# Second layer of a four-layer graph network: 93 of 440 value blocks gathered later, edge one-hots on ScalarE, scaling on two engines

## Chip, cores and metric

The kernel runs on one core of one Trainium2 chip. The metric is device time in microseconds, the median of the runs.

## What is computed

The reference is a network of four layers over 3125 nodes with 256 features and 53,125 edges. Each layer adds a graph part, a mixing part and a feed-forward part to `x`. The change touches only the graph part of the second layer. This is attention over the edges, with 4 heads of 64 features:

```
q, k, v = xn @ Wq + bq (+ query), xn @ Wk + bk, xn @ Wv + bv     # one row of 256 per node
score   = sum over a head of q[dst] * (k[src] + rel_w[relation])   # per edge and head
alpha   = softmax of score over the edges of one dst
out     = segment_sum(alpha * v[src], dst) @ Wo + bo, then a norm with gamma, beta
```

The second line is written from the kernel's own steps; edges are sorted by their destination.

## The kernel before

**The steps.** The sorted edges are cut into `STEPS` = 440 blocks of `W` = 128 edges, one edge per partition; 8 steps are a group (`GROUP`), of which there are 55, and two steps are a pair. A step touches one tile of `P` = 125 destination nodes; there are `NT` = 25 tiles. The function `gnn1` runs five phases one behind the other, with a barrier of all engines between them:

1. `gnn1_front` writes the table `keyval1` to HBM: 3125 rows of 512 numbers, the 256 of the key and then the 256 of the value.
2. `edge_scores` (its tiles are named `g_sc_...` in the profile). GpSimd gathers with an indirect DMA the 128 rows of a step, 2 KB each, into one of 14 slots of `rows` (L3404). SyncE copies the value half of each slot, 128 KB, to a table `kept1` in HBM (L3367), and fetches per group 256 KB of `which` and 250 KB of `near` (L3357, L3358). TensorE spreads the queries of the step's tile over its edges (L3423, three matmuls in bf16) and the relation weights (L3426, L3427). VectorE takes three passes over a pair: add (L3451), multiply (L3455), sum over each head (L3459). GpSimd may fill a slot again when the scores of its pair are made (`scored`) and its value half is stored (`stashed`). Between the pairs TensorE, VectorE and ScalarE also run the layer's mixing part (`mix`, L3117 to L3316), which is spread over the turns.
3. `segment_softmax` (`g_sm_...`) works on the scores alone, through two round trips to HBM. GpSimd has nothing to do in it.
4. `weighted_sums` (`g_sp_...`). SyncE loads the stored values of a step from `kept1` into one of 24 slots (L3618). GpSimd multiplies a pair by `alpha`, 128 partitions by 512 numbers (L3639). ScalarE copies the 8 alphas of a pair beside it (L3630). VectorE makes the one-hot matrix of a step by a comparison (L3657), 8 steps ahead, TensorE multiplies the one-hots and the values (L3650, one f32 matmul of 260 columns, which the profile shows as two), and VectorE adds the bank to the step's tile in `total` (L3665). The comparison reads a ramp that was put into PSUM. One add waits for the one before it (`v.wait_ge(added, s)`), since both may go to one tile.
5. `gnn1_tail` (`g_tail_...`) divides, applies `Wo` and the norm.

The order on every engine is the order in which the code is written; there is no planner. The loops are these:

Of the kernel before, what the change touches and what calls it, by code (L numbers as in the profile page):

```python
# [6 lines left out]
I32 = mybir.dt.int32  # L7
# [3311 lines left out]
def edge_scores(core, name, table, kept, query, relation, factor, scores, heads):  # L3319

# [10 lines left out]
    with Phase(nc, name) as ph:  # L3331
# [8 lines left out]
        const, scaled, numbered, apart, which_set, chain_sem = (ph.sem(n) for n in ("const", "scaled", "numbered", "apart", "which_set", "chain"))  # L3340
        expanded, shifted, multiplied, scored = (ph.sem(n) for n in ("expanded", "shifted", "multiplied", "scored"))
        banks = [ph.ps_pair(f"pair{k}") for k in range(PAIR_BANKS)]
        mix = MemoryMix(core, ph)
        block = ph.block()

        @block.sync
        def _(sp):
            for half in (slice(0, 64), slice(64, 128)):
                sp.dma_start(number[half, :], a["c_types"]).then_inc(const, 16)
                sp.dma_start(rel[half, :], a[relation]).then_inc(const, 16)  # L3350
            mix.load(sp)

            def mark(g):
                if g >= HELD:
                    sp.wait_ge(expanded, GROUP * (g - HELD + 1))
                mine = slice(g * GROUP * W, (g + 1) * GROUP * W)
                sp.dma_start(which[:, g % HELD, :], core.kind_rows[mine].partition_broadcast(128)).then_inc(kind_in[g % HELD], 16)  # L3357
                sp.dma_start(near[:, g % HELD, :], core.near_rows[g, 0:P, :]).then_inc(near_in[g % HELD], 16)  # L3358

            for g in range(HELD):  # L3360
                mark(g)
            for s in range(STEPS):
                k = s % SLOTS
                if s % GROUP == GROUP // 2 and HELD <= s // GROUP + 2 < GROUPS:
                    mark(s // GROUP + 2)
                sp.wait_ge(gathered[k], 16 * (s // SLOTS + 1))
                sp.dma_start(kept[s * W:(s + 1) * W, :], rows[:, k, D:2 * D]).then_inc(stashed[k], 16)  # L3367
            for k in range(SLOTS):
                sp.wait_ge(stashed[k], 16 * ((STEPS - 1 - k) // SLOTS + 1))

        @block.scalar
        def _(act):
# [23 lines left out]

        @block.gpsimd
        def _(pool):
            for s in range(STEPS):
                k = s % SLOTS  # L3400
                if s >= SLOTS:
                    pool.wait_ge(scored, (s - SLOTS) // 2 + 1)
                    pool.wait_ge(stashed[k], 16 * (s // SLOTS))
# [26 lines left out]

        @block.vector
        def _(v):
            nc.vector.memset(one[:], 1.0).then_inc(numbered, 1)
            v.wait_ge(const, 64)
            nc.vector.tensor_scalar(minus[:], number[:], -1.0, None, ALU.mult).then_inc(numbered, 1)
            link = Chain(v, chain_sem).link
# [25 lines left out]
            v.wait_ge(scored, PAIRS)  # L3462


def segment_softmax(core, name, scores, factor, alpha, heads):

# [7 lines left out]
    with Phase(nc, name) as ph:  # L3474
# [19 lines left out]
        banks = [ph.ps(f"bank{i}") for i in range((nv + per - 1) // per)]  # L3494
        turns = [ph.ps(f"turn{i}") for i in range(4)]
        block = ph.block()

        @block.sync
        def _(sp):
# [93 lines left out]
def weighted_sums(core, name, source, alpha, heads, total, own, values):  # L3593

    nc = core.nc
    SLOTS, BANKS, RING, AHEAD = 24, 7, 16, 8
    PAIRS = STEPS // 2  # L3600
    dim = D // heads
    with Phase(nc, name) as ph:
        rows = ph.sb("rows", [W, SLOTS, D + heads])
        same = ph.sb("same", [W, RING, P])
        loaded = [ph.sem(f"loaded{k}") for k in range(SLOTS)]
        cleared, ramped, same_set, scaled, beside, summed, added = (ph.sem(n) for n in ("cleared", "ramped", "same_set", "scaled", "beside", "summed", "added"))
        own_in = ph.sem("own_in")
        banks = [ph.ps(f"bank{k}") for k in range(BANKS)]
        ramp = ph.ps("ramp")
        block = ph.block()  # L3610

        @block.sync
        def _(sp):
            for s in range(STEPS):
                k = s % SLOTS
                if s >= SLOTS:
                    sp.wait_ge(summed, s - SLOTS + 1)
                sp.dma_start(rows[:, k, 0:D], source[s * W:(s + 1) * W, :]).then_inc(loaded[k], 16)  # L3618
                if s % GROUP == GROUP - 1 and s // GROUP < NT:
                    t = s // GROUP  # L3620
                    node_dma(sp, own[:, t, :], nodes(values)[:, t, :], own_in)
            sp.wait_ge(own_in, 32 * NT)

        @block.scalar
        def _(act):
            for pair in range(PAIRS):
                if 2 * pair >= SLOTS:
                    act.wait_ge(summed, 2 * pair + 2 - SLOTS)
                k = 2 * pair % SLOTS
                nc.scalar.activation(rows[:, k:k + 2, D:D + heads], alpha[:, 2 * pair:2 * pair + 2, :], ACT.Copy).then_inc(beside, 1)  # L3630

        @block.gpsimd
        def _(pool):
            for pair in range(PAIRS):
                for s in (2 * pair, 2 * pair + 1):
                    pool.wait_ge(loaded[s % SLOTS], 16 * (s // SLOTS + 1))
                k = 2 * pair % SLOTS
                mine = rows[:, k:k + 2, 0:D].rearrange("p k (h d) -> p k h d", h=heads)
                nc.gpsimd.tensor_tensor(mine, mine, alpha[:, 2 * pair:2 * pair + 2, :].unsqueeze(3).to_broadcast([W, 2, heads, dim]), ALU.mult).then_inc(scaled, 1)  # L3639

        @block.tensor
        def _(pe):
            for s in range(STEPS):
                if s % 2 == 0:
                    pe.wait_ge(scaled, s // 2 + 1)
                    pe.wait_ge(beside, s // 2 + 1)
                pe.wait_ge(same_set, s + 1)
                if s >= BANKS:
                    pe.wait_ge(added, s - BANKS + 1)
                nc.tensor.matmul(banks[s % BANKS][0:P, 0:D + heads], same[:, s % RING, :], rows[:, s % SLOTS, :], start=True, stop=True).then_inc(summed, 1)  # L3650

        @block.vector
        def _(v):
            def compare(s):
                if s >= RING:
                    v.wait_ge(summed, s - RING + 1)
                nc.vector.tensor_scalar(same[:, s % RING, :], ramp[:, 0:P], core.local[:, s:s + 1], None, ALU.is_equal).then_inc(same_set, 1)  # L3657

            def add(s):
                tile = tiles.at(s)  # L3660
                there = total[:, bass.ds(tile, 1), :]
                v.lower_ap(there)
                v.wait_ge(added, s)
                v.wait_ge(summed, s + 1)
                nc.vector.tensor_tensor(there, there, banks[s % BANKS][0:P, 0:D + heads].unsqueeze(1), ALU.add).then_inc(added, 1)  # L3665

            nc.vector.tensor_copy(ramp[:, 0:P], core.ramp[:, 0:P]).then_inc(ramped, 1)
            nc.vector.memset(total[:], 0.0).then_inc(cleared, 1)
            v.wait_ge(ramped, 1)
# [3 lines left out]
            for s in range(AHEAD):  # L3673
                compare(s)
# [282 lines left out]
def gnn1(core):  # L3957
# [2 lines left out]
    table, kept = core.table("keyval1", N, 2 * D), core.table("kept1", STEPS * W, D)  # L3960
    values = table[:, D:2 * D]
    with Phase(nc, "g1") as whole:
        alpha = whole.sb("alpha", [W, STEPS, heads])
        with Phase(nc, "g1b") as outer:
            scores = outer.sb("scores", [W, heads, STEPS])
            with Phase(nc, "g1q") as scope:
                parts = scope.sb("parts", [P, 3, NT, D], BF16)
                gnn1_front(core, table, parts)
                edge_scores(core, "g1_sc", table, kept, parts, "L1_gnn_rel_w", 0.2, scores, heads)
            segment_softmax(core, "g1_sm", scores, dim ** -0.5, alpha, heads)  # L3970
        own, total = whole.sb("own", [P, NT, D]), whole.sb("total", [P, NT, D + heads])
        weighted_sums(core, "g1_sp", kept, alpha, heads, total, own, values)
        gnn1_tail(core, own, total, heads)


# [557 lines left out]
```

## Time and profile before

| what | value |
|---|---|
| runs | 5380.28, 5381.34 and 5816.96 us; median 5381.34 us |
| profiled execution, own time | 5367.56 us |
| its span | 5365.8 us |
| busy in the span | TensorE 77%, VectorE 58%, ScalarE 31%, GpSimd 48% |
| `edge_scores` | from 1609 to 2267 us |
| `segment_softmax` | from 2267 to 2337 us |
| `weighted_sums` | from 2337 to 2619 us |

The phases run one behind the other, so time saved inside one of the last three phases of this table is saved in the whole. An engine's busy share counts overlapping instructions once. For an indirect DMA the busy time on GpSimd is the time in which it prepares the transfer; the data land later. "Idle before" in a group of instructions is the time for which the engine stood still ahead of them, with what ended it.

### The profile page before, as it was taken

The numbers are of one execution on the slowest core, as the hardware profiler recorded it, in microseconds if no ns is written. First come the engines' busy times: TensorE is split into PE (matmuls) and PEld (weight loads), VectorE is DVE, ScalarE is ACT, GpSimd is POOL, SyncE is SP. The second block draws the span as 40 slices with busy tenths as digits, with TensorE's granted clock in tenths as the row PEclk, the third lists the DMA queues.
The fourth block names the chain that finished last, engine by engine and source line by source line (L and its number), as shares of the span: only waits on it lengthen the run. The fifth ranks groups of instructions, "written<-read, shape, count | busy, mean of one in ns | idle before, by whom it ended". The sixth has DMA issues, their size and how long they took to land. (4 is left out here: it accounts for less than half of the span.)

```text
span 5365.8 us, 71878 instructions
## 1 busy us (share of the span) xinstructions
PE 4148.9 (77%) x19209; PEld 3079.2 (57%) x19209; DVE 3099.9 (58%) x7473; ACT 1672.2 (31%) x3813; POOL 2601.8 (48%) x2664
## 2 busy tenths in 40 slices
PE   1689997888976877559859678887499997888674
PEld 1357775656843544334548556666277765566564
DVE  5525546721057788779851467898522225688843
ACT  1345554532231322211333211000233334344221
POOL 1377775502206676548625367775000006777444
PEclk9799998988986777679969889888699999999877
DMA  5344447730028999857332344444100003333434
GB/s 176 117 150 156 155 148 229 220 104 27 31 87 281 328 329 320 268 157 230 91 115 71 95 128 122 122 120 89 48 0 0 0 5 116 103 101 97 94 101 128
DMA packets 463670, 705.71 MB, mean 132 GB/s; under 512 B 70819, under 2 KB 340649, under 8 KB 462923
## 3 DMA queue, kind: packets, MB, share of 16 engines
q0 software_dynamic: 115216, 335.54, 20.8%
q1 hardware_dynamic: 327133, 344.61, 20.5%
q10 hardware_dynamic: 20978, 21.42, 1.3%
q8 instruction: 162, 2.65, 0.2%
q14 instruction: 181, 1.48, 0.1%
HBM read 496.93 MB, written 205.25 MB: 131 GB/s over the span
## 5 line engine op out<-in xcount | busy, mean ns | idle before, releaser
L830 POOL DMA_INDIRECT m_rows<-support,edge x440 | 445.6, 1013 | 878.9 <-POOLq L129 737.1
L3404 POOL DMA_INDIRECT g_sc_rows<-keyval,src_at x440 | 430.3, 978 | 321.0 <-POOLq L129 107.3
L4014 POOL DMA_INDIRECT g_sp_rows<-h,src_at x440 | 469.8, 1068 | 145.9 <-issue 97.2
L2210 POOL DMA_INDIRECT messages<-m_rows,place_at x440 | 429.8, 977 | 154.8 <-issue 96.0
L3423 PE MATMUL g_sc_pair<-g1q_parts,g_sc_near 125*128 x1320 | 289.5, 341 | 145.9 <-DVE g_sc_rows L3455 112.6
L4063 PE MATMUL g_sp_bank<-g_sp_rows,g_sp_same 128*125 128x264 f32 x880 | 287.8, 435 | 73.3 <-DVE g_total L4203 68.7
L1391 DVE SCALAR_TENSOR_TENSOR x<-f_y,f_comb,x 125x256 f32 x200 | 96.8, 484 | 377.9 <-PE f_y L1208 377.9
L851 PE MATMUL m_half<-m_rows,m_marks 128*125 128x256 f32 x880 | 240.8, 408 | 70.3 <-issue 33.6
L3639 POOL TENSOR_TENSOR g_sp_rows<-g_sp_rows,g_alpha 128x512 f32<-128x512 f32 x220 | 225.0, 1043 | 126.2 <-DMA g_sp_rows<-kept 122.7
L1250 ACT ACTIVATE f_hid<-f_h,f_shift,f_scale 128x375 f32<-128x375 f32 (+1 forms) x320 | 195.5, 611 | 288.9 <-PE f_h L1187 283.2
L3650 PE MATMUL g_sp_bank<-g_sp_rows,g_sp_same 128*125 128x260 f32 x880 | 263.5, 421 | 17.2 <-POOL g_sp_rows L3639 10.7
L889 DVE TENSOR_TENSOR g_total<-g_total,m_half 125x256 f32 x440 | 184.7, 420 | 137.8 <-PE m_half L851 120.7
L955 PE MATMUL g_sums_bank<-g_sums_rows,g_sums_marks 128*125 128x256 f32 x880 | 203.1, 387 | 52.4 <-ACT g_sums_marks L946 52.0
L3423 PEld LDWEIGHTS g_sc_pair<-g1q_parts,g_sc_near 125*128 125x128 bf16 x1320 | 126.6, 109 | 197.0 <-issue 161.6
L851 PEld LDWEIGHTS m_half<-m_rows,m_marks 128*125 128x125 f32 x880 | 157.5, 198 | 131.7 <-issue 72.8
L4063 PEld LDWEIGHTS g_sp_bank<-g_sp_rows,g_sp_same 128*125 128x125 f32 x880 | 155.4, 203 | 123.6 <-DVE g_sp_rows L4190 45.3
L3451 DVE TENSOR_TENSOR g_sc_rows<-g_sc_rows,g_sc_pair 128x512 f32<-128x512 f32 x220 | 150.8, 685 | 122.7 <-PE g_sc_pair L3427 53.8
L3650 PEld LDWEIGHTS g_sp_bank<-g_sp_rows,g_sp_same 128*125 128x125 f32 x880 | 132.7, 188 | 147.9 <-issue 98.0
L955 PEld LDWEIGHTS g_sums_bank<-g_sums_rows,g_sums_marks 128*125 128x125 f32 x880 | 162.5, 189 | 92.8 <-ACT g_sums_marks L946 70.3
L973 DVE TENSOR_TENSOR g_total<-g_total,g_sums_bank 125x256 f32 x440 | 185.3, 421 | 48.5 <-PE g_sums_bank L955 34.2
L2244 ACT ACTIVATE m_rows<-m_message,edge 128x256 f32<-128x256 f32 x440 | 178.9, 472 | 82.9 <-PE m_message L2229 82.6
L1457 POOL DMA_INDIRECT xnT<-sorted_rows,f_from_at x160 | 158.9, 993 | 91.0 <-issue 41.8
(734 smaller groups left out, 10425.7 us busy)
## 6 DMA issues: line engine op xcount, KB each, us to landing
g_sums_rows<-messages SPq DMA_DIRECT2D x110, 520.0 KB
kept<-g_sc_rows SPq DMA_DIRECT2D x440, 128.0 KB, 9.1
g_sp_rows<-kept SPq DMA_DIRECT2D x440, 128.0 KB, 2.6
answer_rows<-zero ACTq DMA_DIRECT2D x1, 14592.0 KB
g_sc_which<-kind_rows SPq DMA_DIRECT2D x55, 256.0 KB
m_local_in<-local_rows SPq DMA_DIRECT2D x55, 252.0 KB
near_rows<-m_near SPq DMA_DIRECT2D x55, 252.0 KB
g_sc_near<-near_rows SPq DMA_DIRECT2D x55, 250.0 KB
```

Of the source, the lines that this page charges most:

```text
L830: nc.gpsimd.indirect_dma_start(self.rows[:, k, :], None, self.table, bass.IndirectOffsetOnAxis(ap=core.far_at[:, s:s + 1], axis=0)).then_i ...
L851: nc.tensor.matmul(self.halves[s % slots], self.mark(s), self.rows[:, s % self.SLOTS, :], start=True, stop=True).then_inc(self.summed, 1)
L955: nc.tensor.matmul(halves[s % len(halves)], marks[:, s // GROUP % HELD, s % GROUP, :], rows[:, s % SLOTS, 0:D], start=True, stop=True).the ...
L973: nc.vector.tensor_tensor(there, there, halves[s % len(halves)].unsqueeze(1), ALU.add).then_inc(added, 1)
L1250: nc.scalar.activation(hid[layer][:, i % 2, mo, 0:n], hbank[q % HR][:, 0:n], func, scale=scale[layer][:, g, mo:mo + 1], bias=shift[layer][ ...
L2210: nc.gpsimd.indirect_dma_start(core.messages, bass.IndirectOffsetOnAxis(ap=core.place_at[:, s:s + 1], axis=0), self.rows[:, k, :], None).t ...
L3404: nc.gpsimd.indirect_dma_start(rows[:, k, :], None, table, bass.IndirectOffsetOnAxis(ap=core.src_at[:, s:s + 1], axis=0)).then_inc(gathere ...
L3423: nc.tensor.matmul(banks[pair % PAIR_BANKS][:, s % 2, 0:D], near[:, g % HELD, k * W:(k + 1) * W], query[:, i, bass.ds(tile, 1), :].rearran ...
L3639: nc.gpsimd.tensor_tensor(mine, mine, alpha[:, 2 * pair:2 * pair + 2, :].unsqueeze(3).to_broadcast([W, 2, heads, dim]), ALU.mult).then_inc ...
L3650: nc.tensor.matmul(banks[s % BANKS][0:P, 0:D + heads], same[:, s % RING, :], rows[:, s % SLOTS, :], start=True, stop=True).then_inc(summed, 1)
L4014: nc.gpsimd.indirect_dma_start(self.rows[:, k, :], None, self.table, bass.IndirectOffsetOnAxis(ap=core.src_at[:, s:s + 1], axis=0)).then_i ...
L4063: nc.tensor.matmul(self.banks[s % self.BANKS][0:P, 0:D + self.heads], self.same[:, g % 2, k, :], self.rows[:, s % self.SLOTS, :], start=Tr ...
```

## The change

A new class `Late` names 93 steps: 0 to 23, and from there each sixth (29, 35, ..., 437: 69 of them). For these `edge_scores` gathers only the key half (128 KB instead of 256) and stores nothing; the table is read as 6250 rows of 256 numbers, with indices that VectorE makes at the start of the phase. The values of steps 0 to 23 are gathered by GpSimd during `segment_softmax` into space that `own` takes later, those of the 69 others during `weighted_sums`, each 18 steps ahead of GpSimd's own scaling. The slots there are loaded for steps 24 to 47 at once.

In `weighted_sums` the one-hots are no longer compared by VectorE. ScalarE makes eight squares of (node number - local destination) and one `Relu(1 - square)` over the group. VectorE scales each third pair (pairs 2, 5, 8, ...: 73 in all), GpSimd the other 147. There are 8 banks instead of 7. The diff, cut to what matters:

```
+class Late:
+    EARLY, EVERY = 24, 6
+        self.steps = [t for t in range(STEPS) if t < self.EARLY or t % self.EVERY == self.EVERY - 1]
...
 edge_scores, sync:
+                if s not in late.index:
+                    sp.wait_ge(gathered[k], 16 * (s // SLOTS + 1))
+                    sp.dma_start(kept[s * W:(s + 1) * W, :], rows[:, k, D:2 * D]).then_inc(stashed[k], 16)
 edge_scores, gpsimd:
+            pool.wait_ge(late_set, 2)
...
                     pool.wait_ge(scored, (s - SLOTS) // 2 + 1)
+                    if s - SLOTS not in late.index:
+                        pool.wait_ge(stashed[k], 16 * late.stashes(SLOTS, k, s))
+                if s in late.index:
+                    nc.gpsimd.indirect_dma_start(rows[:, k, 0:D], None, halves, bass.IndirectOffsetOnAxis(ap=late.key(s), axis=0)).then_inc(gathered[k], 16)
+                    continue
...
-    SLOTS, BANKS, RING, AHEAD = 24, 7, 16, 8
+    SLOTS, BANKS, HELD = 24, 8, 3
+    AHEAD, SOONER, THIRD = 18, 3, 3
...
+        def on_vector(pair):
+            return pair % THIRD == THIRD - 1
...
+        def scale(eng, pair):
+            rows_in(eng, pair)
+            mine = there(pair)[:, :, 0:D].rearrange("p k (h d) -> p k h d", h=heads)
+            return eng.tensor_tensor(mine, mine, alpha[:, 2 * pair:2 * pair + 2, :].unsqueeze(3).to_broadcast([W, 2, heads, dim]), ALU.mult)
...
 weighted_sums, scalar:
+                for k in range(GROUP):
+                    s = g * GROUP + k
+                    ins = nc.scalar.activation(mine[:, k, :], core.ramp[:, 0:P], ACT.Square, bias=minus_local[:, s:s + 1])
+                ins.then_inc(apart, 1)
+                act.wait_ge(apart, g + 1)
+                nc.scalar.activation(mine, mine, ACT.Relu, scale=-1.0, bias=one[:, 0:1]).then_inc(same_set, 1)
...
 weighted_sums, gpsimd:
+                if s >= 2 * SLOTS:
+                    pool.wait_ge(summed, s - SLOTS + 1)
+                nc.gpsimd.indirect_dma_start(rows[:, k, 0:D], None, halves, bass.IndirectOffsetOnAxis(ap=late.value(s), axis=0)).then_inc(loaded[k], 16)
...
             for pair in range(PAIRS):
+                for s in (2 * pair + AHEAD, 2 * pair + 1 + AHEAD):
+                    if late.EARLY + AHEAD <= s < STEPS and s in late.index:
+                        gather(s)
+                if not on_vector(pair):
+                    scale(nc.gpsimd, pair).then_inc(pool_scaled, 1)
...
 weighted_sums, vector:
+            for pair in range(SOONER):
+                scale_third(pair)
             for s in range(STEPS):
-                if s + AHEAD < STEPS:
-                    compare(s + AHEAD)
                 add(s)
+                if s % 2 == 0:
+                    scale_third(s // 2 + SOONER)
...
 gnn1:
+        def gather_early(pool):
+            for s in range(late.EARLY):
+                nc.gpsimd.indirect_dma_start(early[:, s, 0:D], None, halves, bass.IndirectOffsetOnAxis(ap=late.value(s), axis=0)).then_inc(early_in, 16)
```

GpSimd in `edge_scores`: where one run of 440 gathers of 512 numbers per row stood, there stand now 24 of 256 numbers, and then one short gather behind each five long ones.

```order
+L3433 DMA g_sc_rows<-keyval,g_late_at 128x256 x24
+L3435 DMA g_sc_rows<-keyval,src_at 128x512 x5
+L3433 DMA g_sc_rows<-keyval,g_late_at 128x256
+L3435 DMA g_sc_rows<-keyval,src_at 128x512 x5
+L3433 DMA g_sc_rows<-keyval,g_late_at 128x256
```

The count of gathers on GpSimd stays at 440 in this phase; only what they move changes.

VectorE at the start of `weighted_sums`, before the change (L809 is the reading of the tile number that an add needs; `g_sp_same` are the one-hots, `g_sp_bank` is what TensorE made):

```order
 L3667 COPY g_sp_ramp<-ramp 128x125
 L3668 MEMSET g_total 125x6500
 L806 TENSOR_LOAD step_tile
 L3657 TENSOR_SCALAR g_sp_same<-g_sp_ramp,local 128x125 x9
 L809 ISA
 L3665 TENSOR_TENSOR g_total<-g_total,g_sp_bank 125x260
 L3657 TENSOR_SCALAR g_sp_same<-g_sp_ramp,local 128x125
```

and after it (`g_own` is the space of the values of steps 0 to 23):

```order
+L3762 TENSOR_SCALAR g_sp_minus_local<-local 128x440
+L3763 MEMSET g_total 125x6500
+L806 TENSOR_LOAD step_tile
+L3675 TENSOR_TENSOR g_own<-g_own,g_alpha 128x2x256
+L809 ISA
+L3755 TENSOR_TENSOR g_total<-g_total,g_sp_bank 125x260
```

One comparison between every two adds is gone; one multiplication of 512 numbers, with both inputs in SBUF, stands behind each six adds.

GpSimd in `weighted_sums`: where 220 multiplications stood in one run (L3639), there are now pairs of them, with a gather between.

```order
+L3721 DMA g_sp_rows<-keyval,g_late_at 128x256 x3
+L3675 TENSOR_TENSOR g_own<-g_own,g_alpha 128x2x256 x8
+L3675 TENSOR_TENSOR g_sp_rows<-g_sp_rows,g_alpha 128x2x256 x2
+L3721 DMA g_sp_rows<-keyval,g_late_at 128x256
+L3675 TENSOR_TENSOR g_sp_rows<-g_sp_rows,g_alpha 128x2x256 x2
```

## Rows read from the trace of the kernel before

**Rows 1.** The page: the span.

```profile
span 5365.8 us, 71878 instructions
```

**Rows 2.** Windows: PE, PEld, DVE, ACT, POOL busy (instructions), PE clock, DMA share, GB/s.

```profile
1640.00:1700.00 60.00, 39.94 (x243) 26.32 (x242) 55.31 (x89) 9.47 (x10) 39.37 (x38) 0.69 0.84 262
1700.00:1950.00 250.00, 198.44 (x1178) 132.79 (x1176) 189.93 (x340) 71.32 (x111) 171.62 (x181) 0.77 0.97 331
1950.00:2250.00 300.00, 209.64 (x1190) 129.46 (x1190) 262.42 (x433) 81.17 (x107) 203.23 (x207) 0.68 0.95 314
2267.00:2337.00 70.00, 11.25 (x38) 7.94 (x38) 32.63 (x76) 8.63 (x10) 0.00 (x0) 0.52 0.18 55
2346.00:2618.00 272.00, 263.37 (x880) 132.50 (x880) 264.98 (x878) 43.37 (x208) 219.88 (x215) 0.99 0.72 218
```

**Rows 3.** Groups, 1600 to 2270 us: busy us, mean ns, idle before and its releasers.

```profile
L3404 POOL DMA_INDIRECT g_sc_rows<-keyval,src_at x440 | 430.3, 978 | 321.0 <-POOLq L129 107.3 <-issue 93.5 <-DMA kept<-g_sc_rows 62.3
```

**Rows 4.** DMA view, 1600 to 2270 us: queue, packets, MB, share of 16 engines.

```profile
q0 software_dynamic: 35200, 115.37, 52.1%
q1 hardware_dynamic: 80184, 88.02, 39.9%
```

**Rows 5.** Timeline, both ends of `edge_scores`: start us, us, engine, line [idle before].

```profile
1625.74 0.94 POOL L3404 DMA_INDIRECT g_sc_rows<-keyval,src_at  x1 [0.30 <-issue]
1631.88 0.82 PE L3423 MATMUL g_sc_pair<-g1q_parts,g_sc_near 125*128 x3 [27.59 <-DMA g_sc_near<-near_rows]
...
1640.85 1.23 POOL L3404 DMA_INDIRECT g_sc_rows<-keyval,src_at  x1 [14.17 <-DMA kept<-g_sc_rows]
...
2252.49 0.95 POOL L3404 DMA_INDIRECT g_sc_rows<-keyval,src_at  x1 [0.30 <-issue]
...
2262.16 0.69 DVE L3451 TENSOR_TENSOR g_sc_rows<-g_sc_rows,g_sc_pair 128x512 f32<-128x512 f32 x1 [0.27 <-issue]
...
2264.55 1.27 DVE L3459 TENSOR_REDUCE g1b_scores<-g_sc_rows 128x8 f32<-128x512 f32 x2
```

**Rows 6.** Groups of `weighted_sums`, and of matmuls in the first layer's sums.

```profile
L3650 PE MATMUL g_sp_bank<-g_sp_rows,g_sp_same 128*125 128x260 f32 x880 | 263.5, 421 | 17.2 <-POOL g_sp_rows L3639 10.7 <-DVE g_total L3665 0.9
L3639 POOL TENSOR_TENSOR g_sp_rows<-g_sp_rows,g_alpha 128x512 f32<-128x512 f32 x220 | 225.0, 1043 | 126.2 <-DMA g_sp_rows<-kept 122.7
L3665 DVE TENSOR_TENSOR g_total<-g_total,g_sp_bank 125x260 f32 x438 | 182.3, 416 | 0.7 <-issue 0.2 <-PE g_sp_bank L3650 0.2
L3657 DVE TENSOR_SCALAR g_sp_same<-g_sp_ramp,local 128x125 f32<-128x125 f32 x440 | 150.5, 344 | 7.0 <-DVE g_total L3668 0.8 <-PE g_sp_bank L3650 0.5 <-issue 0.2
...
L955 PE MATMUL g_sums_bank<-g_sums_rows,g_sums_marks 128*125 128x256 f32 x880 | 203.1, 387 | 52.4 <-ACT g_sums_marks L946 52.0
```

**Rows 7.** Timeline of `weighted_sums`: runs on GpSimd and VectorE, whole time and count.

```profile
2339.15 5.47 DVE L3668 MEMSET g_total<- 125x6500 f32 x1 [1.34 <-issue]
...
2466.66 13.05 POOL L3639 TENSOR_TENSOR g_sp_rows<-g_sp_rows,g_alpha 128x512 f32<-128x512 f32 x13 [0.25 <-DMA g_sp_rows<-kept]
...
2614.17 4.09 DVE L3665 TENSOR_TENSOR g_total<-g_total,g_sp_bank 125x260 f32 x9
```

**Rows 8.** Timeline of `gnn1_tail`: VectorE with GpSimd idle, and with it at work.

```profile
2660.03 0.42 DVE L3948 TENSOR_TENSOR x<-x,g_tail_beta 125x256 f32<-125x256 f32 x1
2660.37 0.42 DVE L3915 TENSOR_TENSOR g_own<-g_tail_out,xw 125x256 f32<-125x256 f32 x1
...
2660.83 0.72 POOL L3848 TENSOR_TENSOR g_own<-g_own,g_tail_gamma 125x256 f32<-125x256 f32 x1 [0.94 <-ACT g_own L3900]
2661.03 0.80 DVE L3948 TENSOR_TENSOR x<-x,g_tail_beta 125x256 f32<-125x256 f32 x1
```

**Rows 9.** Groups on ScalarE: nearest rows to its new work.

```profile
L946 ACT ACTIVATE g_sums_marks<-g_sums_marks,g_sums_one 128x1000 f32<-128x1000 f32 x55 | 62.1, 1128 | 1.8
L3193 ACT ACTIVATE g_sc_mkvrow<-g_sc_mkvrow 125x128 f32<-125x128 f32 x25 | 7.5, 300 | 0.0
L3630 ACT ACTIVATE g_sp_rows<-g_alpha 128x8 f32<-128x8 f32 x220 | 44.7, 208 | 220.5 <-PE g_sp_bank L3650 219.3 <-PEq L129 1.2
```

More of the change, by code:

```diff
@@ L3316, in dve_turn, with __init__, key, value @@
                 nc.vector.tensor_tensor(self.mid[:, k, :], self.banks[t % 2][0:P, D:2 * D], self.b[:], ALU.add).then_inc(self.taken, 1)
-def edge_scores(core, name, table, kept, query, relation, factor, scores, heads):
+class Late:
+    EARLY, EVERY = 24, 6
+    def __init__(self, scope):
+        self.steps = [t for t in range(STEPS) if t < self.EARLY or t % self.EVERY == self.EVERY - 1]
+        self.at = scope.sb("late_at", [W, 2, len(self.steps)], I32)
+        self.index = {t: j for j, t in enumerate(self.steps)}
+    def key(self, t):
+        return self.at[:, 0, self.index[t]:self.index[t] + 1]
+    def value(self, t):
+        return self.at[:, 1, self.index[t]:self.index[t] + 1]
+    def stashes(self, slots, k, until):
+        return len([t for t in range(k, until, slots) if t not in self.index])
+def edge_scores(core, name, table, kept, query, relation, factor, scores, heads, late):
     nc, a = core.nc, core.a
@@ L3342, in edge_scores @@
         banks = [ph.ps_pair(f"pair{k}") for k in range(PAIR_BANKS)]
+        count, first = len(late.steps), next(t for t in late.steps if t >= late.EARLY)
+        twice, late_set = ph.sb("twice", [W, count]), ph.sem("late_set")
+        halves = table.rearrange("n (k d) -> (n k) d", k=2)
         mix = MemoryMix(core, ph)
@@ L3607, in weighted_sums, with there, rows_in @@
         own_in = ph.sem("own_in")
         banks = [ph.ps(f"bank{k}") for k in range(BANKS)]
-        ramp = ph.ps("ramp")
         block = ph.block()
+        def there(pair):
+            s = 2 * pair
+            return early[:, s:s + 2] if s < late.EARLY else rows[:, s % SLOTS:s % SLOTS + 2]
+        def on_vector(pair):
+            return pair % THIRD == THIRD - 1
+        def rows_in(eng, pair):
+            for s in (2 * pair, 2 * pair + 1):
+                if s < late.EARLY:
+                    eng.wait_ge(early_in, 16 * late.EARLY)
+                else:
+                    eng.wait_ge(loaded[s % SLOTS], 16 * (s // SLOTS))
@@ L3625, in _, with match @@
         def _(act):
[L3626 to L3630, printed above, removed]
+            def match(g):
+                mine = same[:, g % HELD]
+                if g >= HELD:
+                    act.wait_ge(summed, GROUP * (g - HELD + 1))
+                for k in range(GROUP):
[4 more added lines that the diff above has]
+                nc.scalar.activation(mine, mine, ACT.Relu, scale=-1.0, bias=one[:, 0:1]).then_inc(same_set, 1)
@@ L3632, in _, with put_beside @@
+            def put_beside(g):
+                for pair in range(g * GROUP // 2, (g + 1) * GROUP // 2):
+                    if 2 * pair >= late.EARLY + SLOTS:
+                        act.wait_ge(summed, 2 * pair + 2 - SLOTS)
+                    nc.scalar.activation(there(pair)[:, :, D:D + heads], alpha[:, 2 * pair:2 * pair + 2, :], ACT.Copy).then_inc(beside, 1)
+            act.wait_ge(placed, 2)
+            for g in range(GROUPS):
+                match(g)
+                put_beside(g)
         @block.gpsimd
@@ L3643, in _ @@
             for s in range(STEPS):
+                pair = s // 2
                 if s % 2 == 0:
-                    pe.wait_ge(scaled, s // 2 + 1)
-                    pe.wait_ge(beside, s // 2 + 1)
-                pe.wait_ge(same_set, s + 1)
+                    mine = len([q for q in range(pair + 1) if on_vector(q) == on_vector(pair)])
+                    pe.wait_ge(dve_scaled if on_vector(pair) else pool_scaled, mine)
+                    pe.wait_ge(beside, pair + 1)
+                if s % GROUP == 0:
+                    pe.wait_ge(same_set, s // GROUP + 1)
```

94 lines of the change are left out of this document (52 added, 42 removed).

## The prediction

> **What bounds the kernel now.** I read the page first for the whole span, 5365.8 us [rows 1], then the windows over the second layer's phases, then the groups and waits inside them, and last the timeline where a pace had to be read. The profiled execution took 5367.56 us, which is 13.8 us under the median of the runs, 5381.34; I sum differences on the profiled one and put them on the median.
>
> In `edge_scores` the DMA engines are busy for 97% of 1700 to 1950 us and 95% of 1950 to 2250 [rows 2]. But nothing else is far off. GpSimd issued 181 gathers in the 250 us of the first stretch, one per 1.381 us, and 207 in the 300 us of the second, one per 1.449. Its own floor is 1.25 us: 0.95 for a gather and 0.30 of idle time behind it [rows 5]. VectorE is busy for 189.93/181 = 1.05 us per step in the first stretch and 262.42/207 = 1.27 in the second; from 1640 to 1700 it is busy 55.31 of 60 us with the DMA at 84% [rows 2]. Of GpSimd's time 93.5 us are its own gaps; of the 62.3 us behind the stores [rows 3], 14.17 are one wait at the start [rows 5]. So DMA limits the middle of the phase, VectorE its first 60 us, and the two together its second half.
>
> In `weighted_sums` VectorE is busy 264.98 of 272 us and waits for nobody, 0.7 and 7.0 us in all [rows 2, 6]. TensorE looks as full, 263.37 us, but it only spreads: the same matmuls, four columns shorter, were busy 203.1 us in the first layer's sums [rows 6]. The phase's pace is 272/440 = 0.618 us per step, 3.7 us for six.
>
> **The change in `edge_scores`.** A step moves 262 KB (128 rows of 2 KB) in, 131 KB out, and (256 + 250) KB/8, some 65 KB, of marks: 458 KB. Check: 331 GB/s by 1.381 us is 457 KB [rows 2]. A late step moves 196 KB. Six steps with one late are 5 x 458 + 196 = 2486 KB, 414 per step, 9.6% less. Bytes are the right measure: per MB the gather queue with 2 KB rows uses 52.1%/115.37 = 0.452% and the other queue, mostly 1 KB rows, 39.9%/88.02 = 0.453% [rows 4]; halving a row does not spoil it.
>
> - Start. The first matmul waits 27.59 us for the first `near`, behind the first gathers, and gather 15 waits 14.17 us until 1640.85 [rows 5]. The first 14 gathers move half and nothing is stored, 14 x 262 KB = 3.7 MB less in the 31 us. GpSimd's wait for the new indices (six small VectorE instructions, some 2 us) delays gathers that nobody wants yet: nothing. VectorE must still do its first pair, so I take -5 (0 to -14).
> - 1640 to 1700: VectorE, at 92%, is the limit: 0.
> - 1700 to 1950: at 331 GB/s, 414 KB take 1.25 us, which is also GpSimd's floor. Two limits at one value never both hold, so I take the middle, 1.31: 181 x 0.07 = -13 (0 to 181 x 0.13 = -24).
> - 1950 to 2250: 414/314 = 1.32 by DMA, 1.27 by VectorE, whose bursts of mixing work can't be filled in later. I take 1.37: 207 x 0.08 = -16 (-5 to 207 x 0.13 = -27).
> - End: from the last gather at 2252.49 to its pair at 2262.16 are 9.7 us [rows 5], with less in the queues some 3 less (0 to -6).
>
> Sum -37 us (-5 to -71).
>
> **`segment_softmax`.** 24 gathers by 1.25 us are 30 us on a GpSimd that did nothing for 70 us, and 3.1 MB on DMA engines at 18% [rows 2]: hidden. The small round trips may meet them: +2 (0 to +6). If that cover were gone, it would be 30 us.
>
> **`weighted_sums`**, per six steps, since the pattern repeats every six.
>
> - VectorE loses the comparisons. An add alone is bound to the one before: nine in 4.09 us, (4.09 - 0.42)/8 = 0.459 us [rows 7]. Six are 2.75. One scaling is a pass over 512 numbers: two such passes took 1.27 us, 0.68 each [rows 5], so one adds 0.59. Sum 3.34.
> - GpSimd: 13 scalings took 13.05 us, 1.0 each [rows 7]. Two, and one gather at 1.25, are 3.25.
> - ScalarE: 8 squares at 0.300 (the nearest row, 128 columns), one wide `Relu` at 1.128, 4 copies at 0.208: 4.36 us for eight steps, 3.27 for six [rows 9]. It works up to two groups ahead, so it hides.
> - TensorE: 203.1/440 = 0.46 per step, 2.8 [rows 6].
> - DMA: 0.72 busy [rows 2], and 3.1 MB have gone into the softmax. The 18 steps between a gather and its scaling by GpSimd leave about 10 steps (6 us) before VectorE wants it, against 9.7 us of landing in a full phase [rows 5]; at 0.72 the queues are short, so I put nothing on it.
>
> So everything would fit into 3.34, were it not for what these two engines do to each other. In the tail VectorE's add of 256 numbers with both inputs in SBUF took 0.42 us with GpSimd idle, and 0.80 when GpSimd's multiplication was under way: it ended 0.28 us behind it. The add with one input in PSUM took 0.42 [rows 8]. Before the change VectorE had no instruction with two SBUF inputs in this phase. Now it has 73. GpSimd scales for 2.0 of each 3.3 us, so a scaling of VectorE meets one in 6 cases of 10 and waits half of it: +0.3 us. If it then goes ahead of GpSimd's second scaling it holds that up by 0.59, in about 3 to 4 cases of 10: +0.2 on 3.25. The longer of the two is 3.64, with a little for unevenness 3.6 to 3.65; against 3.7 I take -0.08 by 73.3 = -6 us.
>
> The Trainium skill ("SBUF — State Buffer", section "Who interferes with whom") says that a VectorE instruction with two SBUF inputs contends with a GpSimd instruction that reads SBUF, and that the one that starts first keeps the shared port for its whole length. By that rule the trace agrees, with 0.42 against 0.80 us. Taken at its worst it gives the third rival's time.
>
> The bounds: below, 3.34, that is -0.36 x 73.3 = -26; above, VectorE waits for a whole scaling each time, 3.34 + 1.04 = 4.38, that is +0.68 x 73.3 = +50. The start is bound by the 5.47 us clearing of `total` [rows 7] as before, and TensorE's first step comes no later: 0.
>
> **The sum**: -37 + 2 - 6 = -41. 5367.56 - 41 = 5326.6 for a profiled execution, 5381 - 41 = 5340 for the median.
>
> **The rivals.**
>
> - *All of it shows.* The saved bytes turn into time to the limits above (-71), and the two scalings fall beside the gathers (-26): -97, 5284. For it: DMA at 95 to 97%. Against: GpSimd's floor stands at the same 1.25, and VectorE's 88% in the second half. Chance 0.13.
> - *The transfer was hidden anyway.* VectorE's bursts and GpSimd's issue take over at once in `edge_scores`, -8, and `weighted_sums` comes out even, with +2 in the softmax: 5375. For it: TensorE's and VectorE's waits on each other in the mixing part. Against: 93.5 us of GpSimd's gaps are the plain 0.30, so it ran unhindered for most gathers. Chance 0.18.
> - *The port decides.* VectorE's scaling waits for a whole one of GpSimd each time, as both run in one rhythm of six steps: +50, with -37 and +2 this is +15, 5396, slower than before. It decides from 3.7 + 35/73.3 = 4.18 us per six steps on. For it: a repeating order has no chance in it, it either always meets or never. Against: when VectorE waits, GpSimd runs on into its gather, which leaves the next meeting open. Chance 0.09.
>
> The forecast has 0.60, with a range of its own from 5320 to 5358.
>
> **How the numbers follow.** The range takes in the second rival (5375) and most of the first (5284), and leaves out most of the third: 5290 to 5382. A measurement of this kernel can tell about 2%, 107 us, from no change. Faster by that needs 5274, beyond even the first rival by 10: 0.05. Slower by it needs 5489, out of reach but for a fault that I don't see, such as gathers that land late for each of 69 pairs at over 1 us: 0.03. The same: 0.92.
>
> **What would show it.** In the trace of the changed kernel: the last gather of `edge_scores` some 35 us earlier, with 1.3 us per gather from 1700 on and the DMA share still over 0.9; waits behind `kept` nearly gone from GpSimd's; the softmax at 70 to 73 us; VectorE's scaling with a mean over 0.9 us instead of 0.68, some at 0.68 and some near 1.5; GpSimd's scaling over 1.04 in the mean; 0.60 us per step. Wrong would be: 0.56 per step with scalings at 0.68 (no meeting), a wait of VectorE on a gather, ScalarE as TensorE's releaser in `weighted_sums`, or a pace of `edge_scores` above 1.38.

## The result and the profile after

The changed kernel takes 5455.61 us in the median of 4 runs (5452.73 to 5461.37), the kernel before 5382.36: a ratio of 1.0131, with a 95% interval from 1.0117 to 1.0145. It is 73 us slower. One of the four runs of the kernel before, 5816.96 us, is in a slower state that some executions show, and the ratio leaves it out. I had forecast 5340 us, in a range up to 5382.

| phase | before | after | forecast |
|---|---|---|---|
| `edge_scores`, first gather to last score | 655.7 us | 624.3 us | -37 |
| `segment_softmax`, with its barrier | 69.9 us | 71.5 us | +2 |
| `weighted_sums`, clearing of `total` to last add | 279.1 us | 381.6 us | -6 |

The three differences are -31, +2 and +103, together +73. (The two profiled executions lie 85 us apart; 10 of it stand ahead of these phases, where the programs are the same, and 1 is the wait of the first gather for the new indices, which the first row leaves out. The first row goes from the start of the first gather to the start of the last score.)

The page's first lines after the change, then the windows over the same phases (span, then busy time of PE, PEld, DVE, ACT and POOL with instructions, PE clock, DMA share, GB/s):

```profile
span 5450.9 us, 71363 instructions
PE 4141.2 (76%) x19209; PEld 3135.2 (58%) x19209; DVE 3176.9 (58%) x7113; ACT 1843.8 (34%) x4308; POOL 2622.5 (48%) x2684
```

```profile
1700.00:1950.00 250.00, 198.73 (x1231) 134.54 (x1231) 205.48 (x367) 73.04 (x112) 181.97 (x191) 0.82 0.97 321
1950.00:2235.00 285.00, 206.64 (x1190) 129.37 (x1190) 253.28 (x421) 78.53 (x105) 196.55 (x202) 0.70 0.92 289
2247.00:2318.00 71.00, 11.47 (x38) 7.96 (x38) 32.71 (x76) 8.63 (x10) 25.52 (x24) 0.50 0.32 98
2327.00:2703.00 376.00, 255.11 (x874) 187.05 (x872) 347.25 (x514) 208.99 (x689) 211.00 (x209) 0.86 0.51 149
```

Against [rows 2]: the first stretch has 191 gathers in 250 us, 1.309 us each, where it had 1.381; the second 202 in 285, 1.41 where it had 1.449. The softmax hides its 24 gathers. The last row is the surprise: VectorE has 364 instructions less than in [rows 2] and is busy 82 us longer. TensorE's granted clock is 0.86 there, where it was 0.99; in e1 below, where TensorE's long waits are gone, it is 0.99 again.

The groups of `weighted_sums` say with what (answering to [rows 6]; busy us, mean ns, idle before and its releasers):

```profile
L3745 PE MATMUL g_sp_bank<-g_sp_rows,g_sp_same 128*125 128x260 f32 x832 | 243.4, 453 | 112.2 <-DVE g_sp_rows L3675 112.2
L3755 DVE TENSOR_TENSOR g_total<-g_total,g_sp_bank 125x260 f32 x440 | 185.9, 423 | 27.8 <-PE g_sp_bank L3745 12.5 <-DVE g_total L3755 3.3
...
L3675 DVE TENSOR_TENSOR g_sp_rows<-g_sp_rows,g_alpha 128x512 f32<-128x512 f32 x69 | 164.0, 2377 | 0.0
L3675 POOL TENSOR_TENSOR g_sp_rows<-g_sp_rows,g_alpha 128x512 f32<-128x512 f32 x139 | 142.0, 1047 | 1.4
L3699 ACT ACTIVATE g_sp_same<-ramp,g_sp_minus_local 128x125 f32<-128x125 f32 x440 | 133.4, 386 | 146.5 <-PE g_sp_bank L3745 145.3 <-DVE g_sp_minus_local L3762 1.2
...
L3721 POOL DMA_INDIRECT g_sp_rows<-keyval,g_late_at x69 | 68.1, 987 | 186.7 <-PE g_sp_bank L3745 146.8 <-POOLq L129 39.1 <-issue 0.8
```

A pass of VectorE over 512 numbers took 0.68 us in [rows 5]. Its scalings take 2377 ns in the mean. GpSimd's are as they were, 1047 ns. The timeline shows one cycle of six steps (start, duration, engine and line; several instructions in one row have their count behind x):

```profile
2456.03 0.99 POOL L3721 DMA_INDIRECT g_sp_rows<-keyval,g_late_at  x1 [2.03 <-PE g_sp_bank L3745]
2457.04 2.04 POOL L3675 TENSOR_TENSOR g_sp_rows<-g_sp_rows,g_alpha 128x512 f32<-128x512 f32 x2
2457.11 2.53 DVE L3675 TENSOR_TENSOR g_sp_rows<-g_sp_rows,g_alpha 128x512 f32<-128x512 f32 x1
...
2459.57 2.70 DVE L3755 TENSOR_TENSOR g_total<-g_total,g_sp_bank 125x260 f32 x6
...
2459.70 4.56 PE L3745 MATMUL g_sp_bank<-g_sp_rows,g_sp_same 128*125 128x260 f32 x12 [2.19 <-DVE g_sp_rows L3675]
...
2461.11 0.98 POOL L3721 DMA_INDIRECT g_sp_rows<-keyval,g_late_at  x1 [2.03 <-PE g_sp_bank L3745]
2462.12 2.05 POOL L3675 TENSOR_TENSOR g_sp_rows<-g_sp_rows,g_alpha 128x512 f32<-128x512 f32 x2
2462.19 2.53 DVE L3675 TENSOR_TENSOR g_sp_rows<-g_sp_rows,g_alpha 128x512 f32<-128x512 f32 x1
```

VectorE starts its scaling at 2457.11, 0.07 us behind GpSimd's first, and ends it at 2459.64. GpSimd's two scalings end at 2459.08; the rest, 0.56 us, is the scaling itself. So VectorE does not get in between the two. The next cycle follows 5.08 us later with the same lengths, to 0.01 us. In the record of the whole phase 65 of VectorE's 73 scalings are long, and each of the 65 ends 0.55 or 0.56 us behind the last of the GpSimd scalings that it met. Even clearer is the start of the phase, where GpSimd has ten scalings in a row:

```profile
2322.75 8.04 POOL L3675 TENSOR_TENSOR g_own<-g_own,g_alpha 128x512 f32<-128x512 f32 x8
2326.64 6.70 DVE L3675 TENSOR_TENSOR g_own<-g_own,g_alpha 128x512 f32<-128x512 f32 x1 [0.76 <-DVE g_total L3763]
2330.76 2.03 POOL L3675 TENSOR_TENSOR g_sp_rows<-g_sp_rows,g_alpha 128x512 f32<-128x512 f32 x2
```

The scaling that VectorE began in the fourth of them ended at 2333.34, 0.55 us behind the tenth.

The cycle can be added up from the rows above. VectorE's scaling ends at 2459.64. TensorE, which waited for it, starts 0.06 us later, the gather 1.41 us after that, and GpSimd's scalings 1.01 us after the gather. They take 2.05 us, and VectorE's next scaling ends 0.55 us behind them: 5.08 us. The code says why the gather comes just there. The gather of step t waits until TensorE has done step t - 24, and because 24 slots are four times the period of six, that step is always the second of a pair that VectorE scales.

My theory after this: (a) VectorE's instruction with two SBUF inputs does not get in before the end of a whole back-to-back run of GpSimd; (b) the meeting is no chance: TensorE waits for VectorE's scaling, GpSimd's gather waits for a slot that TensorE frees with the second step of that same pair, and the two scalings follow the gather, just when VectorE has done its six adds. The rivals: the gather's wait for its slot alone makes the cycle; the eight or six banks do; or VectorE loses against any scaling whatever the phase.

### The profile page after: what moved, and what is told of

Read it like the earlier page. It is cut to its first block and busy times, and to the rows that moved or that the text cites. A ratio compares the mean times of both kernels' runs of the same rounds, so it can differ in the third digit from the quotient of the medians.

```text
span 5450.9 us, 71363 instructions
## 1 busy us (share of the span) xinstructions
PE 4141.2 (76%) x19209; PEld 3135.2 (58%) x19209; DVE 3176.9 (58%) x7113; ACT 1843.8 (34%) x4308; POOL 2622.5 (48%) x2684
## 5 line engine op out<-in xcount | busy, mean ns | idle before, releaser
L3435 POOL DMA_INDIRECT g_sc_rows<-keyval,src_at x347 | 334.7, 965 | 141.9 <-issue 78.7
L3745 PE MATMUL g_sp_bank<-g_sp_rows,g_sp_same 128*125 128x260 f32 x832 | 243.4, 453 | 112.2 <-DVE g_sp_rows L3675 112.2
L3745 PEld LDWEIGHTS g_sp_bank<-g_sp_rows,g_sp_same 128*125 128x125 f32 x832 | 178.1, 220 | 177.3 <-DVE g_sp_rows L3675 143.0
L4164 PEld LDWEIGHTS g_sp_bank<-g_sp_rows,g_sp_same 128*125 128x125 f32 x880 | 153.5, 200 | 122.6 <-DVE g_sp_rows L4291 46.9
L2229 PE MATMUL m_message<-far_parts,m_near 125*128 x1320 | 182.6, 279 | 30.7 <-ACT m_rows L2244 19.1
```

The source lines that it names most:

```text
L4164: nc.tensor.matmul(self.banks[s % self.BANKS][0:P, 0:D + self.heads], self.same[:, g % 2, k, :], self.rows[:, s % self.SLOTS, :], start=Tr ...
```

## The experiments

All but e9 are edits of the changed kernel. e1 to e4 ran where the kernel before takes 5380.3 us, e5 to e8 where it takes 5845.6, e9 to e12 where it takes 5798.3; each is compared with those. e2, e3, e4, e6, e8, e9 and e12 are single runs; of them I use the length of a phase in the trace rather than the whole time.

**e1, the factors in PSUM.** At the start VectorE copies its 73 pairs' alphas to two banks, 0.9 us, and reads them there; the copy is not shown.

```
-    SLOTS, BANKS, HELD = 24, 8, 3
+    SLOTS, BANKS, HELD = 24, 6, 3
+        factors = [ph.ps(f"factor{k}") for k in range(2)]
...
-            return eng.tensor_tensor(mine, mine, alpha[:, 2 * pair:2 * pair + 2, :].unsqueeze(3).to_broadcast([W, 2, heads, dim]), ALU.mult)
+            by = factor_of(pair) if on_vector(pair) else alpha[:, 2 * pair:2 * pair + 2, :]
+            return eng.tensor_tensor(mine, mine, by.unsqueeze(3).to_broadcast([W, 2, heads, dim]), ALU.mult)
```

> VectorE's 73 scalings read their factors from PSUM, so they have one input in SBUF; the banks go from 8 to 6 to make room. Port theory (VectorE waits while GpSimd scales): each scaling falls from a median of 2.5 us to 0.68, six steps take about 3.4 us instead of 5.08, weighted_sums falls from 384 to about 265 us and the kernel to about 5335. Rival, the gather's slot wait (GpSimd waits 146.8 us for TensorE before its gathers and that sets the rhythm): scalings get short but the cycle stays near 5 us and the kernel near 5450.

Measured: 5342.20 us, ratio to before 0.9927 (0.9898 to 0.9955); `weighted_sums` 259.0 us. The timeline, and VectorE's group:

```profile
2452.42 2.04 POOL L3682 TENSOR_TENSOR g_sp_rows<-g_sp_rows,g_alpha 128x512 f32<-128x512 f32 x2
2452.60 0.68 DVE L3682 TENSOR_TENSOR g_sp_rows<-g_sp_rows,g_sp_factor 128x512 f32<-128x512 f32 x1
```

```profile
L3682 DVE TENSOR_TENSOR g_sp_rows<-g_sp_rows,g_sp_factor 128x512 f32<-128x512 f32 x69 | 46.9, 680 | 0.0
```

The scaling runs inside GpSimd's and takes 0.68 us. It saves 164.0 - 46.9 = 117 us of VectorE's time, and some 6 at the phase's start; the phase is 123 us shorter. That is more than the 103 us that the phase had lost. Part of it may be the two banks fewer, which e2 tests.

**e2, six banks alone**, the control (`BANKS` 8 to 6).

> Control for e1: 6 banks instead of 8 and nothing else. Both theories: TensorE runs less far ahead of the adds, weighted_sums stays within 10 us of 384, scalings of VectorE still at a median over 2 us.

Measured: 5446.46 us, `weighted_sums` 367.2 us, the scalings' median 2156 ns. Six banks make the phase 14 us shorter (I had allowed 10); VectorE's 69 scalings take 150.0 us instead of 164.0. The other 108 of e1's 123 us are the input that moved to PSUM, so the second input in SBUF is what the change paid for.

**e3, GpSimd waits for its own last scaling.**

```
                 if not on_vector(pair):
+                    if pair:
+                        pool.wait_ge(pool_scaled, len([q for q in range(pair) if not on_vector(q)]))
                     scale(nc.gpsimd, pair).then_inc(pool_scaled, 1)
```

> GpSimd waits for its own last scaling before it starts the next, so its two scalings no longer stand back to back. If the port is held over a whole back-to-back run, VectorE's scaling gets in behind the first one: about 1.6 us instead of 2.5, cycle about 4.2 us (GpSimd's second scaling is then pushed back by 0.6), weighted_sums about 315 to 325 us. If the port is given per instruction anyway and VectorE merely loses each time, it stays at 2.5 and 5.08 us per six steps.

Measured: 5380.14 us, beside 5380.3 for before; `weighted_sums` 302.3 us, better than expected.

```profile
2454.44 2.51 POOL L3675 TENSOR_TENSOR g_sp_rows<-g_sp_rows,g_alpha 128x512 f32<-128x512 f32 x2
2454.90 1.15 DVE L3675 TENSOR_TENSOR g_sp_rows<-g_sp_rows,g_alpha 128x512 f32<-128x512 f32 x1
```

VectorE asks at 2454.90, in the first scaling, and is done at 2456.05; GpSimd's two now take 2.51 us instead of 2.04. So between two scalings that are not back to back VectorE gets in. One added wait, with nothing else changed, takes 79 us off the phase. This shows (a). What happens between two back-to-back scalings, whether GpSimd keeps its hold or takes it again before VectorE can, no run tells apart: in the changed kernel's record GpSimd's second scaling starts 0.05 us before the end of the first, in e3's 0.08 us behind it.

**e4, the gather 12 steps ahead instead of 18** (`AHEAD`).

> GpSimd gathers 12 steps ahead of itself instead of 18, so that the slot has been free for 6 more steps and the gather does not wait for TensorE. If the rhythm (the gather's wait starts both scalings just when VectorE has done its six adds) makes the loss, the meetings spread: mean scaling near 1.4 us, cycle near 4.0, weighted_sums 290 to 310 us. If any run of scalings hits VectorE whatever the phase, it stays near 384. If the gathers now land late, VectorE or GpSimd waits for the DMA.

Measured: 5448.46 us, `weighted_sums` 368.5 us: my expectation fell.

```profile
2451.22 0.98 POOL L3721 DMA_INDIRECT g_sp_rows<-keyval,g_late_at  x1 [2.03 <-PE g_sp_bank L3745]
2452.22 2.04 POOL L3675 TENSOR_TENSOR g_sp_rows<-g_sp_rows,g_alpha 128x512 f32<-128x512 f32 x2
2452.30 2.52 DVE L3675 TENSOR_TENSOR g_sp_rows<-g_sp_rows,g_alpha 128x512 f32<-128x512 f32 x1
```

The gather waits 2.03 us as before. GpSimd has some 3 us of work in a cycle of 5.08, so it runs ahead until its slots are used up, whatever `AHEAD` says, and the slot of a late step is always freed by the same one of six steps. Besides, 12 and 18 differ by one whole cycle, so the gather stands at the same place between GpSimd's scalings. This distance moves no phase; a distance that is no multiple of six was not run.

**e5, VectorE scales four pairs ahead** (`SOONER` 3 to 4).

> VectorE scales its pair 4 pairs ahead instead of 3, that is behind the add two steps earlier in the cycle of six. In the changed kernel GpSimd's two scalings start 0.07 us before VectorE asks. If that order alone makes the loss (phase theory), VectorE now asks 0.9 us earlier and goes first: its scaling 0.68 us for most, cycle 3.4 to 3.7 us, weighted_sums 255 to 275 us, kernel 5335 to 5355. Rival (GpSimd's scalings find VectorE whatever the phase): median scaling stays over 2 us and the kernel near 5450.

Measured: 5931.25 us against 5845.57, ratio 1.0142 (1.0112 to 1.0172), `weighted_sums` 375.6 us. The "order alone" form of my theory fell.

```profile
2751.39 0.98 POOL L3721 DMA_INDIRECT g_sp_rows<-keyval,g_late_at  x1 [2.03 <-PE g_sp_bank L3745]
2752.40 2.04 POOL L3675 TENSOR_TENSOR g_sp_rows<-g_sp_rows,g_alpha 128x512 f32<-128x512 f32 x2
2752.85 2.15 DVE L3675 TENSOR_TENSOR g_sp_rows<-g_sp_rows,g_alpha 128x512 f32<-128x512 f32 x1
...
2755.05 3.25 PE L3745 MATMUL g_sp_bank<-g_sp_rows,g_sp_same 128*125 128x260 f32 x12 [1.78 <-DVE g_sp_rows L3675]
...
2756.47 0.98 POOL L3721 DMA_INDIRECT g_sp_rows<-keyval,g_late_at  x1 [2.03 <-PE g_sp_bank L3745]
2757.47 2.04 POOL L3675 TENSOR_TENSOR g_sp_rows<-g_sp_rows,g_alpha 128x512 f32<-128x512 f32 x2
2757.92 2.15 DVE L3675 TENSOR_TENSOR g_sp_rows<-g_sp_rows,g_alpha 128x512 f32<-128x512 f32 x1
```

The reason is in these rows. VectorE's scaling ends at 2755.00; TensorE, which waited for it, starts at 2755.05; the gather is released at 2756.47 and GpSimd's scalings start at 2757.47, 2.47 us behind the end of VectorE's. VectorE has six adds before its next scaling, wherever in the six its scaling stands. It asks 2.92 us behind the end of the last one here, 0.41 us sooner in the cycles without the wait that about every second one has. Both lie within the 2.47 to 4.51 us in which GpSimd scales. As long as TensorE waits for the scaling, both engines count from its end, and they meet: 61 of the 69 scalings here took over 2 us, 63 of 69 in the changed kernel.

**e6, five pairs ahead.**

> Five pairs ahead: the scaling stands two more steps earlier, so VectorE asks 1.8 us before GpSimd's scalings, or if the whole pattern has shifted, 1 us behind their start. Phase theory: either 0.68 us and a cycle of 3.4 to 3.7 (kernel near 5345), or a wait of about 1.1 us and a cycle near 4.4 (weighted_sums 325, kernel near 5400). Rival: as the changed kernel, 5450.

Measured: 5860.55 us against 5845.57; `weighted_sums` 285.6 us.

```profile
2755.01 0.98 POOL L3721 DMA_INDIRECT g_sp_rows<-keyval,g_late_at  x1 [0.16 <-issue]
2756.01 2.05 POOL L3675 TENSOR_TENSOR g_sp_rows<-g_sp_rows,g_alpha 128x512 f32<-128x512 f32 x2
...
2758.45 0.68 DVE L3675 TENSOR_TENSOR g_sp_rows<-g_sp_rows,g_alpha 128x512 f32<-128x512 f32 x1
2759.06 2.71 DVE L3755 TENSOR_TENSOR g_total<-g_total,g_sp_bank 125x260 f32 x6
```

```profile
L3675 DVE TENSOR_TENSOR g_sp_rows<-g_sp_rows,g_alpha 128x512 f32<-128x512 f32 x69 | 66.5, 964 | 0.0
```

What TensorE waited for in e5, and then in e6 (from the lists of waits: microseconds in total, times, longest):

```profile
PE g_sp_bank L3745 <- DVE g_sp_rows L3675: 84.2, 51, 7.1
```

```profile
PE g_sp_bank L3745 <- DVE g_total L3755: 21.0, 50, 5.0
```

The same instructions, the same inputs in SBUF, and the phase is 90 us shorter than e5's, measured at the same place. With eight banks TensorE can be at most eight steps ahead of the adds, and five pairs are ten steps, where e5's four pairs were just eight: it waits for banks now and no longer for `g_sp_rows` from VectorE. In the cycle shown VectorE's scaling falls into the gather, and the cycle is 3.24 us. Not all are like it: 38 of the 69 scalings took 0.68 or 0.69 us, 27 met one scaling of GpSimd, and 4 met a longer run. So the meetings are no longer the rule once TensorE does not wait. This shows (b).

**e7, both: factors in PSUM and five pairs ahead.**

> Factors in PSUM and VectorE's scaling five pairs ahead. In e1 the cycle was 3.60 us with TensorE waiting 0.31 us for VectorE's scaling each time and VectorE waiting 0.41 us for TensorE, because three pairs ahead is too late. If that is all that is left, the cycle becomes 3.34 us (six adds 2.75 and 0.59), weighted_sums about 250 us and the kernel about 5323. Rival: GpSimd, at 3.03 us of work per cycle, or ScalarE (3.5 us by its waits in e1) keeps it at 3.5 to 3.6: about 5340.

Measured: 5819.51 us against 5845.57, ratio 0.9947 (0.9929 to 0.9966); `weighted_sums` 258.5 us, as e1. The expected 250 did not come. From the first add to the end of the last are 251.3 us in e1 and 250.8 here, 3.42 us per six steps, 2% over VectorE's own 3.34; the 3.60 that I had read in e1 was one stretch. With the contention gone there is nothing left for the distance to win. The 0.41 us that I had taken for a wait for TensorE is something else. In e1 36 of the 440 adds wait about 0.41 us, each the fourth of a group of eight, and each has just ahead of it the reading of the next eight tile numbers (L806), 0.60 us. Before the change no add waited for it: a comparison stood between every two adds. The views put this wait down to TensorE.

**e8, only steps 0 to 23 late.**

```
-        self.steps = [t for t in range(STEPS) if t < self.EARLY or t % self.EVERY == self.EVERY - 1]
+        self.steps = [t for t in range(STEPS) if t < self.EARLY]
```

> Only steps 0 to 23 are late; the 69 others are stored and loaded as before, so GpSimd gathers nothing in weighted_sums and does 147 scalings there. edge_scores: if its gain came from fewer bytes, it goes from 629 back to about 655 us from the first phase instruction on. weighted_sums: if the gather's wait for its slot is what ties GpSimd's scalings to TensorE's steps, the meetings scatter and the scaling's median falls below 1.7 us (phase near 330 us); if GpSimd's lead is always cut by its slots, whoever loads them, the scalings are released by landing loads one by one and VectorE waits for at most one: about 1.2 us, phase near 300.

Measured: 5827.02 us against 5845.57; `weighted_sums` 276.7 us.

```profile
L3674 DVE TENSOR_TENSOR g_sp_rows<-g_sp_rows,g_alpha 128x512 f32<-128x512 f32 x69 | 66.0, 957 | 0.0
```

```profile
POOL g_sp_rows L3674 <- DMA g_sp_rows<-kept: 103.6, 84, 6.8
```

The second fence is from the list of waits: microseconds in total, times, longest. Without the gathers GpSimd waits 84 times for a load, its scalings meet VectorE's less, and the mean falls from 2377 to 957 ns. Its `edge_scores` takes 777.6 us, within 4 us of e7's 773.7 with 93 late steps, which speaks against my "fewer bytes" there. The kernel before was not profiled at this place, so e9 to e11 take up the question elsewhere.

**e9 to e11, `edge_scores` beside each other**: the kernel before unedited; e1's kernel with only 24 late steps; e1's kernel again.

> The kernel before, unedited, profiled on the chip of the next three. It gives the length of edge_scores, the softmax and weighted_sums without the change, for e10 and e11 to stand beside.

> Only steps 0 to 23 late, factors in PSUM. If the gain of edge_scores comes from bytes not moved, it is in proportion to the late steps: against e9 the time from the first gather to the last score falls by about a quarter of what e11 shows (24 of 93). If instead the start alone (late near table, first gathers) makes it, e10 gains as much as e11. weighted_sums about 255 to 265 us, since the port is out of it.

> Factors in PSUM with all 93 late steps, as e1. On a chip like that of the first runs: edge_scores 25 to 30 us shorter than e9, weighted_sums (from the clearing of total to the last add) 259 us. On a chip like that of e5 to e8, where gathers are slower, I expect edge_scores to gain less than 10 us, and weighted_sums the same 259.

Measured: 5794.06 us; 5776.85, ratio 0.9962 (0.9946 to 0.9978); 5781.73, ratio 0.9972 (0.9952 to 0.9991). First gather to last score took 758.8, 766.5 and 760.1 us: no gain from 24 or from 93. What both kernels win over before, 21 and 17 us, is the 20 us of `weighted_sums`. e10's proportion can't be read where there is nothing to share out. `weighted_sums` took 278.8, 258.4 and 258.4 us, the same as on the first chip. The windows of e9 and of e11 in the middle of the phase:

```profile
2100.00:2300.00 200.00, 139.53 (x735) 87.79 (x735) 148.26 (x248) 50.86 (x69) 121.26 (x122) 0.64 0.89 275
```

```profile
2100.00:2300.00 200.00, 143.21 (x711) 87.69 (x710) 147.03 (x244) 49.25 (x66) 115.90 (x118) 0.60 0.82 242
```

A gather takes 1.64 and 1.69 us here, against 1.4 before on the first chip, and the DMA engines were at 0.89 and fall to 0.82 when fewer bytes are asked of them. So on this chip the DMA engines' time was not the limit, and taking bytes away gave none back. The waits of e9 differ from those of the first chip: GpSimd stood 165.0 us behind VectorE's scores (57.9 on the first chip) and 13.1 behind the stores (62.3), and VectorE's first pass 98.8 us behind a DMA (34.3), which by the code can only be the gather, and 97.4 behind TensorE (53.8). So gathered rows came late for VectorE more than on the first chip, although the DMA engines had time left. Why stays open.

**e12, all scaling on GpSimd.** `on_vector` returns False.

> GpSimd scales all 220 pairs and gathers the 69 late steps; VectorE only adds; ScalarE makes the one-hots as in the change. Sum of GpSimd's rows: 220 x 1.0 + 69 x 1.0 to 1.25 = 289 to 306 us, so weighted_sums 295 to 315 us: over the 279 of before and under the 381 of the change. That would show that handing a third to VectorE in this form costs more than it takes off GpSimd.

Measured: 5833.06 us against 5798.3; `weighted_sums` 303.6 us.

```profile
L3675 POOL TENSOR_TENSOR g_sp_rows<-g_sp_rows,g_alpha 128x512 f32<-128x512 f32 x208 | 210.9, 1047 | 1.2
L3755 DVE TENSOR_TENSOR g_total<-g_total,g_sp_bank 125x260 f32 x440 | 186.9, 425 | 111.2 <-PE g_sp_bank L3745 72.9 <-DVE g_total L3755 16.9 <-issue 4.5
```

As summed from the rows. VectorE stands idle for 111.2 us, and still the phase is 78 us shorter than with its help in the change's form. (The 381.6 us are from the first chip; the phase took 279.1 and 278.8 us on the two for before, 259.0 and 258.4 for e1's kernel.)

## Why the prediction was wrong

- **`edge_scores`: right, with its size.** Forecast -37, measured -31, or -30 with the wait for the indices. The start gave 6 us up to gather 15 (25.3 us against 31.4), for my 5. The two paces were 1.31 and 1.37; they came out at 1.309 and 1.41, and GpSimd's 62.3 us behind the stores [rows 3] are 10.4. The second half gave less back than I took; that VectorE's bursts are the reason is argued, not shown. That there is no gain on the chip of e9 to e11 was in no part of the forecast, so the size is right for the first chip alone.
- **The softmax: right.** +2 forecast, +2 measured. The gathers are hidden.
- **The engines' own sums in `weighted_sums`: right.** With the contention out (e1), 3.42 us per six steps against my 3.34, and ScalarE and TensorE are no limit. I had left out the reading of the tile numbers, 36 waits of 0.41 us. e1 gains 20 us over before in this phase; my lower bound was 26.
- **The step that failed is the one on what VectorE and GpSimd do to each other.** I had seen in [rows 8] that a two-input instruction of VectorE waits behind GpSimd's, and priced it as half of one scaling in 6 cases of 10, +0.3 us a cycle, with one whole scaling each time, +1.04, as the upper bound. Measured, a scaling took 2377 ns in the mean in place of 680, so the term that I had put at 0.3 us a cycle was 1.7. Two things in it were wrong. The wait is not for one instruction but for what is left of the whole back-to-back run: up to 2.04 us here, 6.15 at the start, shown by e3. In the tail, where I read it, GpSimd's instructions wait between each other, so that a single one is the longest run that can be seen. And the meeting is not random: TensorE waits for the scaling and frees the slot that GpSimd waits for, so it comes in 63 of 69 cycles and not in 6 of 10 (e4 and e5 against e6). 164.0 us of scalings in place of 46.9, and the slow start, are the whole difference between this phase and e1's.
- **The third rival** had the right engine, place and sign, and even the reason for certainty, one rhythm of six steps. I gave it +50 where the phase lost 103, for the same reason, and 0.09, because I held that GpSimd would run on into its gather. It does not run on; it waits there for the slot, 146.8 us in all. My range up to 5382 left most of this rival out, and even its own time of 5396 was 60 us too low.
- By the rule of the Trainium skill that I had cited ("SBUF — State Buffer", section "Who interferes with whom"), the wait would end with GpSimd's one instruction. The rows show it end with the run (2.53 us, and 6.70 at the start); the measurement decides.
- I had given 0.92 to a time within 2% of before, and 1.3% slower lies within. That is luck rather than insight: 2% of this kernel is 107 us, and the phase that I called nearly even lost 103 of them.

## What to carry to other kernels

Before giving VectorE a part of GpSimd's elementwise work, count the inputs in SBUF on VectorE's side: with two, price a meeting at the length of GpSimd's longest back-to-back run, not of one instruction. Put one input into PSUM if a bank is free; here that turned +73 us into -38. If none is, one wait between GpSimd's instructions lets VectorE in; here that gave all of the 73 us back. Where a producer works a fixed distance ahead, make the distance longer than the consumer's banks allow it to lead (ten steps against eight banks in e6). Otherwise, as here, its waits can put both engines into one rhythm, and what collides once collides in nearly every cycle. By the code the 24 slots, a multiple of the period of six, tie the gather to VectorE's pair as well; another number of slots was not run.

## What the runs showed of the hardware that I had not expected

- A VectorE instruction with two SBUF inputs waited through the rest of a run of ten GpSimd multiplications, from the fourth to the end of the tenth (6.70 us for a pass of 0.68). A semaphore wait between two GpSimd instructions was enough to let it in: 1309 ns in the mean in e3 against 2377.
- The same gathers run at different paces on different chips: 1.4 us per step and a DMA share of 0.95 to 0.97 on one, 1.64 us and 0.89 on another, while single instructions of VectorE and GpSimd took the same time on both (680 ns for a pass, 946 and 947 ns for issuing a gather). A saving of bytes was worth 31 us on the one and nothing on the other.
- The version of e1 is faster than the kernel before on both chips where it ran: 0.9927 and 0.9972 of its time, by less than 1%.
